# Layer 1 attention: where a chunk's output is turned and split among the next heads' steps

## What is computed

```python
qkv = x @ w_attn + b_attn
q, k, v = jnp.split(qkv, 3, axis=-1)
q, k, v = (heads(q), heads(k), heads(v))          # 16 heads of 32
att = jnp.einsum('bhqd,bhkd->bhqk', q, k) * scale
att = jnp.where(causal, att, -jnp.inf)
att = jax.nn.softmax(att, axis=-1)
y = jnp.einsum('bhqk,bhkd->bhqd', att, v)
y = y.transpose(0, 2, 1, 3).reshape(Bsz, Tlen, Cdim)
return y @ w_proj + b_proj
```

## Time and profile before

| | |
|---|---|
| median of 3 runs | 2153.31 us (2149.83 to 2153.51) |
| the profiled execution, its own time | 2150.08 us |
| its span, first to last instruction | 2148.4 us |
| PE busy | 1905.7 us (89%) |
| DVE busy | 1603.8 us (75%) |
| ACT busy | 1362.4 us (63%) |
| POOL busy | 1130.4 us (53%) |
| mean granted clock of PE | 0.957 |
| 15 turns of the output | 1470.8 to 1868.8 us |

### The profile page before, as it was taken

How to read it: one execution, slowest core, us unless ns; L and a number is a source line. 1 busy time by engine, 2 the same in 40 slices (tenths; PEclk the granted TensorE clock), 3 DMA queues, 4 the chain that set the end, 5 groups by cost and what they waited for, 6 DMA issues and landing times. The chain is left out here.

```text
span 2148.4 us, 40251 instructions
## 1 busy us (share of the span) xinstructions
PE 1905.7 (89%) x14509; PEld 1186.3 (55%) x14509; DVE 1603.8 (75%) x3518; ACT 1362.4 (63%) x3320; POOL 1130.4 (53%) x877
## 2 busy tenths in 40 slices
PE   0789999999999999999996799777898989878999
PEld 0455566566666666666665465445666666633444
DVE  7799988888888887888763599657778687834760
ACT  6587777777767767777753244256867676835442
POOL 5687786776776776666640489543323132200440
PEclk9899999999999999999997899978999999989999
DMA  5333331322213212343215844374434243345100
GB/s 179 123 114 128 114 108 56 117 70 70 84 65 94 75 69 75 113 138 109 82 52 189 338 155 146 136 256 152 130 114 134 92 136 126 111 145 179 40 20 20
DMA packets 106861, 249.88 MB, mean 116 GB/s; under 512 B 10480, under 2 KB 39280, under 8 KB 104624
## 3 DMA queue, kind: packets, MB, share of 16 engines
q1 hardware_dynamic: 83872, 190.49, 26.5%
q10 hardware_dynamic: 19680, 46.67, 6.3%
q0 software_dynamic: 3120, 10.23, 1.6%
HBM read 175.26 MB, written 68.94 MB: 114 GB/s over the span
## 5 line engine op out<-in xcount | busy, mean ns | idle before, releaser
L996 PE MATMUL ps_q<-a_y,a_w 128*128 128x512 f16 x1536 | 343.8, 381 | 58.3 <-POOL a_y L691 57.7
L996 PEld LDWEIGHTS ps_q<-a_y,a_w 128*128 128x128 f16 x1536 | 147.6, 98 | 226.3 <-issue 60.9
L714 POOL TENSOR_TENSOR a_rb<-a_rb,router_y 128x512 f32<-128x512 f32 x128 | 181.8, 1420 | 167.2 <-ACT a_rb L857 166.4
L1210 DVE TENSOR_REDUCE a_nmax<-ps_s 128x1 f32<-128x512 f32 (+3 forms) x256 | 123.8, 484 | 111.2 <-PE ps_s L1017 111.1
L1005 PE MATMUL ps_v<-a_w,a_y 128*128 128x128 f16 x3072 | 182.9, 220 | 0.0
L856 ACT ACTIVATE a_rb<-ps_q 64x512 f32<-64x512 f32 x128 | 76.0, 593 | 168.7 <-DVE a_ra L1195 167.1
L1043 PE MATMUL ps_o<-a_tt_,a_v 128*128 128x512 f32 (+3 forms) x512 | 157.0, 451 | 25.5 <-ACT a_tt_ L899 22.2
L1005 PEld LDWEIGHTS ps_v<-a_w,a_y 128*128 128x128 f16 x3072 | 175.2, 98 | 1.2
L1065 PE MATMUL ps_v<-a_o,a_wo 128*128 128x512 f16 x732 | 168.0, 379 | 1.9 <-ACT a_v L883 1.9
L876 ACT ACTIVATE ps_s<-ps_s,a_nmax 128x512 f32<-128x512 f32 (+3 forms) x256 | 125.1, 489 | 39.8 <-DVE a_nmax L1212 39.7
L2211 ACT ACTIVATE a_ef<-ps,a_nmax 128x512 f32<-128x512 f32 (+3 forms) x256 | 131.7, 535 | 26.6 <-DVE a_nmax L2575 25.1
(11 more groups left out here) (344 smaller groups left out, 4977.6 us busy)
## 6 DMA issues: line engine op xcount, KB each, us to landing
a_w<-wqkv_split SPq DMA_DIRECT2D x48, 768.0 KB, 4.5
scratch_numlog<-wkv_nl ACTq DMA_DIRECT2D x40, 512.0 KB, 2.8
wkv_kt<-in_fT ACTq DMA_DIRECT2D x56, 256.0 KB, 2.7
router_y<-in_wqkv SPq DMA_DIRECT2D x16, 768.0 KB, 5.4
wqkv_split<-a_w SPq DMA_DIRECT2D x16, 768.0 KB, 6.9
a_stacks<-qk_parts SPq DMA_DIRECT2D x96, 128.0 KB, 2.6
gate_up<-in_gate_up SPq DMA_DIRECT2D x8, 1408.0 KB, 17.5
a_nlc<-scratch_numlog SPq DMA_DIRECT2D x17, 512.0 KB, 5.1
```

The costliest lines, as they stand in the source:

```text
L714: pool.tensor_tensor(rb[:, n, :], rb[:, n, :], rot[:, 2 * n + 1, :], ALU.mult).then_inc(s["roped"], 1)
L996: mm = pe.matmul(psq[n][:], w16[:, g % 2, wp, n, c, :], y16[b % 2][:, yp, c, :], start=c + m == 0, stop=c == CC - 1 and m == 2)
L1210: dve.tensor_reduce(nmax[:, 0, j:j + 1], cols(ps, j), AX, ALU.max, negate=True)
```

## The change

In head i = 1, PE turns the output behind `turn(h)`, not ahead of it; ACT takes its high half behind `turned_high(h)`; DVE takes its low half behind `turned_low(h)`. Waits and operations are the same ones, and `output(1)` of the head i = 3 keeps its place in the order.

```diff
 # ACT
                             if final(b) and i == 0:
                                 ff_raw(q)
+                            more = not final(b) or q + 1 < CC
+                            turned_high(h, i)
                             if i == 1 and (q or not first):
                                 ot_high(it - 1, (q - 1) % CC)
-                            more = not final(b) or q + 1 < CC
-                            turned_high(h, i)
                             if more or i + 1 < HPC:
                                 exps(h + 1, i + 1)
 # PE
+                            if last_output:
+                                pe.wait_ge(s["x3"], (b - 1) * CC + 1)
+                                output(1)
+                            turn(h, i)
                             if i == 1 and (q or not first):
                                 if more:
                                     pe.wait_ge(s["q"], it + 2)
                                 else:
                                     pe.wait_ge(s["vf"], it + 1)
                                 turn_output(it - 1, q + 1)
-                            if last_output:
-                                pe.wait_ge(s["x3"], (b - 1) * CC + 1)
-                                output(1)
-                            turn(h, i)
 # DVE
-                            if i == 1 and (q or not first):
-                                ot_low(it - 1, (q - 1) % CC)
...
                             turned_low(h, i)
+                            if i == 1 and (q or not first):
+                                ot_low(it - 1, (q - 1) % CC)
```

## The result

The change makes the kernel slower: the median is 2182.93 us (2180.22 to 2189.01, 4 runs) against 2152.14 us before (2149.83 to 2153.51, 4 runs). The ratio is 1.0151, its 95% interval 1.0127 to 1.0174. The profiled execution has a span of 2178.6 us where it was 2148.4, 30.2 us more.

What follows compares the result with a forecast made beforehand. The prediction took layer 1's k projection, on which PE, ACT and DVE hang, as the bound. From 2150.1 us, 22.8 us of order and 6.7 of clock gave 2179.6, so a median of 2180 us, range 2164 to 2192.

Steps and rivals of the forecast that it cites:

- The bound: Layer 1 attention: PE, ACT and DVE all hang on the k projection; DVE's wait before the output's low half is mostly slack.
- order term: Layer 1's chunks: later starts of the k projection, passed whole to the layer's end, make the kernel 22.8 us slower.
- ordinary chunk: Six layer 1 chunks, log term done about when the output's turn starts: k projection 1.62 us later each, 9.7 us.
- first chunk: Layer 1's first chunk, DVE's maxima held behind a DMA: k projection starts at 1482.28, not 1478.97, 3.3 us later.
- five chunks that go by ACT's or PE's side: Layer 1 chunks with DVE ready early: k projection 1.32 to 1.49 us later each, 6.9 us in all.
- last chunk's gain of 0.4 us: Layer 1's last chunk, without k projection: ACT's copy no longer precedes the next exponentials' inputs, 0.4 us gained.
- clock term: PE's new waits before the k projections lower its granted clock: 6.7 us slower, ends 0 and 18.6 us.
- Five falls: Two thirds of eight chunks with 2.2 to 3.3 us PE waits drop to half clock, 1.33 us each.
- (b): Rival, layer 1: delay partly absorbed, PE's 17.4 us of waits for DVE's a_t go, 2162 us; chance 0.09.
- (c): Rival, layer 1: k projection has room, the waits only change names, 2150 to 2153 us; chance 0.04.
- (d): Rival: DVE sets layer 1's pace, earlier maxima gain 19.5 us, 2130.6 us; chance 0.05.
- (a): Rival: every new PE wait halves the clock, fourteen k projections cost 18.6 us, total 2191.5 us; chance 0.12.

Runs made afterwards that it cites:

- added wait: Kernel before the change, nothing moved, PE's k projection also waiting for the next head's maxima: 2174.7 us against 2154.22, ratio 1.0108.
- filler: The change plus five overwritten 128x512 matmuls on PE ahead of the values in 14 chunks: 2168.91 us, ratio 1.0092 against the kernel before.

## Why the prediction was right

*The bound.* The k projection was named as the link on which three engines hang. The added wait alone shows it: 17.9 us of delay in the k projections and 3.1 of slowness gave 21.8 us in the span.

*The order term.* I gave 23.2 us to the 14 chunks and measured 21.2. An ordinary chunk has 1.52 us where I had 1.62, because the maxima start 0.08 us ahead of the log term's recorded end and the hand-over to PE takes 0.72 us, not 0.75; the first chunk has 2.96 for 3.3. The five chunks that go by ACT's or PE's side have most of the difference: 1.04 to 1.38 us, 6.0 together, where I had 1.32 to 1.49 and 6.9. The last chunk's gain of 0.4 us was never isolated.

*The clock term.* Five falls were forecast and five slow k projections found, but one of them had been slow before. The price was too low: I took 1.33 us for a fall from one row, and the five cost 1.15 (on top of the slow one of before), 2.55, 1.70, 1.34 and 1.70 us; with hundredths in the other nine that is 8.6 for 6.7. The mistake was to read a single row of a projection that was slow in part of its length; 5.30 us against 2.77 shows what a whole slow one costs. Filling part of the stand took the term away. That the number of falls came out at five is in part luck: it was two thirds of eight, from three waits. The Trainium skill (TensorE: Matmul & The Clock Gate, HAM oscillation) has the loop that goes cold in every burst. The change is not there, with 9 of 14 at full clock, but the kernel with ACT's part undone nearly is, with 12 of 14 slow behind 2.75 us or more. What that page says of transposes was not tried by any run.

*The sum.* 22.8 + 6.7 = 29.5 us were forecast for the profiled execution and 30.2 found. That it is this close is luck: the order term was 1.9 us too high and the clock term 1.9 too low. Outside the two terms, the time between the chunks grew by 4.2 us (2.2 of it in the waits for the DMA) and the time behind the last take of k fell by 3.7. The second piece is 296 to 300 us in all eleven kernels, so its fall is not the change's alone; neither was forecast or followed up.

*The rivals.* That nothing behind the k projection has room held: PE's wait for a_t before scores did not shrink (17.4 us before, 18.6 now), and (b) falls. (c) and (d) fall with the waits: the low half's 30 us were slack, as the run with the low half behind the maxima shows by itself. (a), 18.6 us for the clock, was too dear for this kernel and about right for the one with ACT's part undone (18.4). DVE's wait at a_yf was forecast at some 50 us and is 61, since a slow k projection lengthens it as well; with filler, where none is slow, it is 51.5.

## What to carry to other kernels

A long wait is worth removing only if what the engine does next is waited for. Follow the hand-over to the end, here to the matmuls that need the single bank back, and price an edit by when these may start. When work is moved behind other work on one engine, look at who waits for the moved piece: a subtraction of 0.69 us, put behind 3.2 us of other work ahead of 14 k projections, cost thirty. And a new stand on PE may cost more than its length, so count the clock in it.

## What the runs showed of the hardware

I had not expected how steeply the share of slow k projections rises with the length of PE's stand ahead of them. Behind stands of 0.1 to 1.4 us (the change with filler) 0 of 14 were slow. Behind 1.2 to 3.1 us (the change, 27.6 us in 14) 5 were, and behind 2.75 us or more (ACT's part undone, 40.1 us in 14) 12 were. Standing 45% longer took the price of the slow k projections from 8.6 to 18.4 us.

Over all eleven kernels, with the first of the 14 chunks left aside, none of the 117 k projections behind at most 1.4 us of standing was slow, and 18 of the 26 behind 1.6 us or more were. The length of the stand alone doesn't decide: of the change's four behind 2.11 us two were slow and two not. Nor is a stand right ahead needed: the first chunk's k projection was slow in the kernel before, at a granted clock of 0.70, with no idle time of PE directly before it.

With the filler PE did more work, and the kernel was 14 us faster than the change, 9.6 of them by the clock of the k projections.
